# The band's factor on the fourth pair too, shared by GpSimd and VectorE, with the values moved behind the third scores

## What is computed

```
q = (x @ Wq.T + bq + ocr_bias)   k, v likewise     # 16 heads of width 8
scores = q·k / sqrt(8)
scores += 0.1 where |i - j| <= 2, else 0           # the band
attn = softmax(scores)                             # over the 256 keys
out = (attn · v) @ Wo.T + bo
```

## Time and profile before

| | us |
|---|---|
| median of 3 runs | 464.08 |
| the runs | 457.72, 464.08, 465.10 |
| the profiled execution | 460.4 |
| its span | 458.4 |
| mean granted clock | 0.981 |
| TensorE busy in the span | 413.9 (90%) |
| VectorE busy | 348.8 (76%) |
| GpSimd busy | 298.3 (65%) |
| ScalarE busy | 284.8 (62%) |

### The profile page before, as it was taken

One profiled execution on the slowest core, in us unless ns is written; L12 is line 12 of the kernel. 1 busy time (PEld: TensorE's weight loads), 2 busy tenths in 40 slices (PEclk: granted clock), 3 DMA queues, 4 the chain that ended last, 5 costly groups with the idle time before them and its releaser, 6 DMA issues.

```text
span 458.4 us, 11229 instructions
## 1 busy us (share of the span) xinstructions
PE 413.9 (90%) x3804; PEld 265.9 (58%) x3804; DVE 348.8 (76%) x878; ACT 284.8 (62%) x523; POOL 298.3 (65%) x569
## 2 busy tenths in 40 slices
PE   8999789999999998897879888899999999887996
PEld 3555436666666654454447564567667766544674
DVE  5878766888778766996699986767788878367992
ACT  5886424666676676687886448055547575777732
POOL 5523625777777772357899647245676789779962
PEclk9999988999999999899899999989999999999999
DMA  7001876323224100000000006983343332000001
GB/s 215 2 1 49 203 211 166 107 77 85 88 73 104 55 4 1 2 0 2 0 1 2 1 1 165 234 224 93 80 104 107 82 80 56 5 0 1 23 24 46
DMA packets 31123, 31.82 MB, mean 69 GB/s; under 512 B 4953, under 2 KB 26329, under 8 KB 31074
## 3 DMA queue, kind: packets, MB, share of 16 engines
q1 hardware_dynamic: 31074, 31.18, 25.6%
HBM read 21.30 MB, written 9.44 MB: 67 GB/s over the span
## 4 chain that ended last, share of the span: by engine, by line
PE 49%; DVE 18%; POOL 15%; issue 8%; ACT 8%; DVEq 0%; POOLq 0%; ACTq 0%
PE psum L722 6%; ACT h_sb L349 4%; DVE nm L821 4%; POOL hq L1496 3%; PE psum L672 3%; PE psum L675 3%; PE psum L703 3%; PE psum L693 2%; PE psum L673 2%; POOL hb_v L1491 2%; PE psum L726 2%; DVE xn L240 2%; PE psum L694 2%; PE psum L660 2%; DVE nm L824 2%
## 5 line engine op out<-in xcount | busy, mean ns | idle before, releaser
L771 ACT ACTIVATE h_sb<-psum 128x1024 f32<-128x1024 f32 (+1 forms) x128 | 110.9, 914 | 45.9 <-PE psum L694 25.5
L821 DVE TENSOR_REDUCE nm<-psum 128x2 f32<-128x512 f32 x128 | 81.7, 684 | 15.0 <-PE psum L673 14.5
L824 DVE TENSOR_REDUCE nm<-psum 128x3 f32<-128x384 f32 x128 | 65.6, 551 | 10.8 <-PE psum L679 8.9
L781 POOL TENSOR_TENSOR h_sb<-h_sb,bandw 128x512 f32<-128x512 f32 x45 | 57.2, 1271 | 0.0
L246 POOL TENSOR_TENSOR rstd<-veps,mhalf 128x4 f32<-128x4 f32 (+1 forms) x29 | 27.7, 954 | 39.9 <-DVE veps L232 38.8
L722 PE MATMUL psum<-h_sb,v_b 128*32 128x256 f32 x512 | 40.9, 391 | 3.4 <-POOL h_sb L785 1.7
L785 POOL TENSOR_SCALAR_AFFINE_SELECT h_sb<-h_sb 128x512 f32<-128x512 f32 x64 | 40.8, 637 | 0.0
L672 PE MATMUL psum<-kst,qst 72*128 72x256 bf16 x128 | 33.9, 282 | 2.9 <-DMA kst<-k_dram 1.2
L858 DVE RECIPROCAL rsum<-psum 128x16 f32<-128x16 f32 x32 | 8.2, 256 | 33.7 <-PE psum L738 33.7
L675 PE MATMUL psum<-kst,qst 72*128 72x128 bf16 x128 | 29.1, 227 | 5.0 <-DVE nm L824 3.1
L673 PE MATMUL psum<-kst,qst 72*128 72x256 bf16 x128 | 33.3, 276 | 0.0
(11 more groups left out here) (256 smaller groups left out, 1176.2 us busy)
## 6 DMA issues: line engine op xcount, KB each, us to landing
qst<-q_dram SPq DMA_DIRECT2D x96, 96.0 KB
kst<-k_dram SPq DMA_DIRECT2D x96, 96.0 KB
q_dram<-q_parts SPq DMA_DIRECT2D x16, 192.0 KB, 2.6
k_dram<-k_parts SPq DMA_DIRECT2D x16, 192.0 KB, 2.8
k_dram<-k_parts SPq DMA_DIRECT2D x16, 128.0 KB, 2.9
x<-in_L_attn_x SPq DMA_DIRECT2D x4, 256.0 KB, 4.3
out_x<-x SPq DMA_DIRECT2D x4, 256.0 KB, 2.3
pk<-in_packed SPq DMA_DIRECT2D x1, 689.5 KB, 5.9
```

Source lines behind the costliest of these rows:

```text
L771: nc.scalar.activation(pexp[p][:, :, 0:w], psum[:, 4 + 2 * (p % 2):6 + 2 * (p % 2), 0:w], ACT.Exp, scale=scale).then_inc(sem("a_exp"), 1)
L781: ins = nc.gpsimd.tensor_tensor(wide, wide, bandw[:].unsqueeze(1).unsqueeze(1).to_broadcast([P, 2, 2, P]), ALU.mult)
L821: nc.vector.tensor_reduce(nm[slot % 2][:, HEAD[h]], bank[e].rearrange("p (t k) -> p t k", t=2), AX.X, ALU.max, negate=True).then_inc(sem(" ...
L824: nc.vector.tensor_reduce(nm3[slot % 2][:, HEAD[h]], bank[e][:, 0:3 * P].rearrange("p (t k) -> p t k", t=3), AX.X, ALU.max, negate=True).t ...
```

## The change

- `MASKED` becomes (4, 4). Pair 3 of the first attention has 2 products of 256 columns a head, as the others do. The two bf16 copies of the band (`bandm`, `bandm2`) and the ScalarE instructions that make them go.
- GpSimd multiplies the first head of pair 3, behind mask 2 and ahead of the split. VectorE multiplies the second head, one unit later, behind the first pair's maxima (and y) and ahead of the second pair's.
- In unit 15 VectorE does all four pairs; unit 14's second half is in its queue ahead of them.
- The values of group 1 wait for both engines' semaphores, and move behind the third scores.

```diff
-        MASKED = (3, 4)
+        MASKED = (4, 4)
...
-                    if l0 and p < MASKED[inst]:
+                    if l0:
                         nc.tensor.matmul(ps[:, 0:S], k[:, 0:P], q[:, 0:S], start=True, stop=True)
                         last = nc.tensor.matmul(ps[:, S:2 * S], k[:, P:S], q[:, 0:S], start=True, stop=True)
-                    elif l0:
-                        nc.tensor.matmul(ps[:, 0:P + BAND], k[:, 0:P], q[:, 0:P + BAND], start=True, stop=False)
-                        nc.tensor.matmul(ps[:, 0:P + BAND], identb[:], bandm[:], start=False, stop=True)
...
                 if l0 and isinstance(qd, int) and (qd, slot) == last_slot:
-                    pe.wait_ge(sem("a_mskd"), min(2 * g + 2, MASKED[inst]))
+                    pe.wait_ge(sem("a_mskd"), 15 + 2 * g + 2)
                 else:
...
+                    pe.wait_ge(sem("a_msk"), m0 + MASKED[inst] * 4 * (qd - q0) + (MASKED[inst] * slot + 2 * g + 2))
+                    if l0 and g == 1:
+                        pe.wait_ge(sem("a_mskd"), 4 * qd + (slot + 1))
...
+            def banded(p, es):
+                n = es.stop - es.start
+                wide = pexp[p].rearrange("p e (t c) -> p e t c", c=P)[:, es, 0::3]
+                edge = pexp[p][:, :, P:3 * P].rearrange("p e (t c) -> p e t c", c=BAND)[:, es, 0::P - 1]
+                return (wide, bandw[:].unsqueeze(1).unsqueeze(1).to_broadcast([P, n, 2, P]),
+                        edge, bande[:].unsqueeze(1).to_broadcast([P, n, 2, BAND]))
...
                 if l0:
+                    wide, by_wide, edge, by_edge = banded(p, slice(0, 1 if p == 3 else 2))
+                    nc.gpsimd.tensor_tensor(edge, edge, by_edge, ALU.mult)
+                    ins = nc.gpsimd.tensor_tensor(wide, wide, by_wide, ALU.mult)
...
+            def dve_mask(dve, qd, slot, p, es):
+
+                dve.wait_ge(sem("a_exp"), PR * 4 * qd + (PR * slot + p + 1))
+                wide, by_wide, edge, by_edge = banded(p, es)
+                nc.vector.tensor_tensor(edge, edge, by_edge, ALU.mult)
+                nc.vector.tensor_tensor(wide, wide, by_wide, ALU.mult).then_inc(sem("a_mskd"), 1)
...
                         pe_scores(eng, *n2, 1, opening, 2)
-                    if has_prev and l0:
-                        pe_values(eng, *prev, 1)
                     if has_2:
                         pe_scores(eng, *n2, 2, opening, 2)
-                    if has_prev and not l0:
+                    if has_prev:
                         pe_values(eng, *prev, 1)
...
                         dve_y(eng, *yb)
+                    if has_prev and l0:
+                        dve_mask(eng, *prev, 3, slice(1, 2))
                     if has_2:
                         dve_max(eng, *n2, 1)
...
                     if final_band:
-                        dve_mask(eng, 0)
-                        dve_mask(eng, 1)
+                        dve_mask(eng, qd, slot, 0, slice(0, 2))
+                        dve_mask(eng, qd, slot, 1, slice(0, 2))
                     if has_prev:
                         dve_norm(eng, *prev)
                     if final_band:
-                        dve_mask(eng, 2)
+                        dve_mask(eng, qd, slot, 2, slice(0, 2))
+                        dve_mask(eng, qd, slot, 3, slice(0, 2))
```

More of the change, by code:

```diff
@@ L80, in build @@
         identb = sb("identb", [P, P], bf16)
-        bandm = sb("bandm", [P, P + BAND], bf16)
-        bandm2 = sb("bandm2", [P, P + BAND], bf16)
         bandw = sb("bandw", [P, P])
@@ L713, in pe_values @@
                 if l0 and isinstance(qd, int) and (qd, slot) == last_slot:
-                    pe.wait_ge(sem("a_mskd"), min(2 * g + 2, MASKED[inst]))
+                    pe.wait_ge(sem("a_mskd"), 15 + 2 * g + 2)
                 else:
-                    pe.wait_ge(sem("a_msk"), m0 + MASKED[inst] * 4 * (qd - q0) + (MASKED[inst] * slot + min(2 * g + 2, MASKED[inst])))
-                if 2 * g + 2 > MASKED[inst]:
-                    pe.wait_ge(sem("a_exp"), PR * 4 * qd + (PR * slot + 2 * g + 2))
+                    pe.wait_ge(sem("a_msk"), m0 + MASKED[inst] * 4 * (qd - q0) + (MASKED[inst] * slot + 2 * g + 2))
+                    if l0 and g == 1:
+                        pe.wait_ge(sem("a_mskd"), 4 * qd + (slot + 1))
                 out = [bank[2][32 * c:32 * c + 32, 0:S] for c in range(4)]
@@ L771, in act_exp @@
                 nc.scalar.activation(pexp[p][:, :, 0:w], psum[:, 4 + 2 * (p % 2):6 + 2 * (p % 2), 0:w], ACT.Exp, scale=scale).then_inc(sem("a_exp"), 1)
+            def banded(p, es):
[4 more added lines that the diff above has]
+                        edge, bande[:].unsqueeze(1).to_broadcast([P, n, 2, BAND]))
             def pool_mask(pool, qd, slot, p):
-                if p >= MASKED[inst]:
-                    return
                 pool.wait_ge(sem("a_exp"), PR * 4 * qd + (PR * slot + p + 1))
                 if l0:
[L778 to L781, removed]
+                    wide, by_wide, edge, by_edge = banded(p, slice(0, 1 if p == 3 else 2))
+                    nc.gpsimd.tensor_tensor(edge, edge, by_edge, ALU.mult)
+                    ins = nc.gpsimd.tensor_tensor(wide, wide, by_wide, ALU.mult)
                 if not l0:
@@ L1744, in biases @@
                 nc.scalar.activation(maskqk[:], mask_f[:], ACT.Copy)
-                nc.scalar.activation(bandm[:], band_f[:, BAND:P + 2 * BAND], ACT.Copy)
                 nc.scalar.activation(bandw[:], band_f[:, BAND:P + BAND], **gain)
                 nc.scalar.activation(bande[:, 0], band_f[:, P + BAND:P + 2 * BAND], **gain)
-                nc.scalar.activation(bande[:, 1], band_f[:, 0:BAND], **gain)
-                nc.scalar.activation(bandm2[:], band_f[:, 0:P + BAND], ACT.Copy).then_inc(sem("c_masks"), 1)
+                nc.scalar.activation(bande[:, 1], band_f[:, 0:BAND], **gain).then_inc(sem("c_masks"), 1)
                 eng.wait_ge(sem("c_q"), 2)
```

## The result

| | before | changed |
|---|---|---|
| median of 5 runs, us | 463.54 | 492.16 |
| lowest to highest | 457.72 to 465.10 | 486.84 to 502.46 |
| ratio, 95% interval | | 1.0641 (1.0569 to 1.0712) |
| span of the profiled execution | 458.4 | 495.6 |
| mean granted clock, profiled | 0.981 | 0.916 |

The forecast was 478, from 464 to 490; the ratio, here and in the experiments, leaves out executions more than 1.5% above the fastest of their kernel, here the profiled one (497.53) and one of 502.46.

The account below looks back on a forecast made before the run. TensorE's queue was taken to bound each unit. Waits net of shorter products +12.9, units 0, 14 and 15 -0.5 and the stage's end +3 gave +15.4 us; on 462.2 that is 478, range 464 to 490.

Parts of the forecast that it names:

- The wait behind the second scores: TensorE, units 1 to 13: third scores wait for banks, 1.09 us (even) or 1.39 (odd); +12.9 net of shorter products.
- The end of the stage: Units 14 and 15: values of group 1 wait for VectorE's half, and VectorE has more mask work; +3 us, 1.1 to 4.9.
- the wait behind y: Unit 15: VectorE's half is queued behind y, so the values of group 1 start 2.2 us later.
- The shorter products: Pair 3's scores on TensorE: four products replace twelve, saving 0.26 us a unit, 4.2 us at most.
- rival 1: Odd units: VectorE's half loses the SBUF collision and waits for GpSimd's mask; +8.8 us, 487; chance 0.18.
- the term for TensorE's granted clock: TensorE's clock might fall in the third scores' waits; named as a sign of error, not in the sum.
- Rivals 2 and 3: Units' waits: 2, they replace others, 458 us, chance 0.10; 3, about half remains, 469 us, chance 0.12.

Follow-up runs that it names:

- the values back: The changed kernel with only the values of group 1 put back ahead of the third scores: 1.014 of the kernel before, 1.004 when measured again.
- filled kernel: The changed kernel with nine unused identity products a unit in TensorE's waits before and between the third scores' heads: 479.2 us, 1.039 of the kernel before.

## Why the prediction was wrong

The direction was right, the mechanism of the largest term was right and its size a little too large, the time was out of the range by 2 us, and a whole term was missing.

- The wait behind the second scores. Forecast were 1.09 us in even units and 1.39 in odd ones; the trace has 1.10 and 1.33 in units 6 and 5, and 1.13 and 1.24 in units 4 and 3. Two units at full clock were to take 16.2 and take 15.85, 1.65 more than the 14.2 before. The rest is small waits that went: TensorE had stood for about 0.1 us ahead of each unit's transposed maxima, and with the values in front of them it no longer does. That makes +10.7 over 13 units, where 12.9 was worked out.
- The end of the stage. +3 was forecast, from 1.1 to 4.9. With the values back it is 2.8 by the traces and 3.4 by the ratios, by the steps that were named, the wait behind y above all. With the values moved it is more. In the filled kernel the last transposed maxima to the last y take 18.4 us, 3.7 more than before; the two units ahead of that take 14.4 for 12.4, of which one unit's wait explains 0.8. That is 4.9 in all, the forecast's upper bound, and the clock is at the lower level for 7 us of it. What was not seen is that GpSimd's half mask prolongs the hold on the layer norm's scaling.
- The shorter products. 0.26 us a unit, right (two units 14.2 to 13.7).
- VectorE's half and the collision (rival 1). VectorE came first in the odd units as long as the clock was full, and lost twice at half clock, by 2 us in all. Rival 1 is not what took the time past 483. The row that spoke for it was misread: in the earlier trace rows VectorE did not come first by 0.11, since GpSimd's edge had been running from 172.25, before VectorE's 172.30. There too the engine that came first went through.
- The sum with the clock nearly full. The filled kernel at a clock of 0.985 took 473.56, the kernel before at 0.988 on that chip 457.98: +15.6. The sum of the prediction was +15.4. That it agrees so closely is luck: the waits were put 2.2 too high and the end 1.9 too low.
- The step that failed is the term for TensorE's granted clock, which the sum puts at nothing. The last sentence of the prediction names it ("or if TensorE's granted clock falls in these waits, which the stage before doesn't show and the sum doesn't hold"), without a price or a chance. The clock does fall. The reason given was wrong as well, since the kernel before shows it at the lower level within this stage, in unit 0:

```profile
65.50:72.00 6.50, 6.50 (x27) 3.52 (x25) 3.40 (x6) 2.31 (x3) 3.14 (x5) 0.50 0.69 193
```

- The price of the clock. The kernel before's own executions give it: 457.52 us at 0.992 and 465.24 at 0.971, 3.7 us for each 0.01. For the 0.04 lost that is 15 us. Measured are 29.7 (0.0641 × 463.5) less 15.6, so 14.
- Rivals 2 and 3 rested on VectorE catching up. It doesn't: the third scores waited in every unit from 1 to 13, at either level of the clock.

Shown by the runs is that the long stretch at half clock comes with the wait and the shorter products together, with no half on VectorE and no factor on pair 3, that the wait alone brings a smaller one, and that it goes when three products fill the wait. Part of why the clock still varies from 0.97 to 0.99 between executions is a fall at the beginning of the stage, near 65 us: in seven of the thirteen profiled executions it lasts 7 to 14 us, in the other six it is missing. Why it comes in some and not in others stays open, and so does what decides when a stretch at the lower level ends.

## What to carry to other kernels

Products that stand in front of a wait for a bank are cover. Before moving them, take the starts of the instructions that read the bank and count when it comes free. Where TensorE is the slowest engine, a wait in every unit has two prices: its length at full clock, and what the clock takes if it falls; a few idle products put into the wait tell the two apart. A factor moved to another engine at a stage's end also lands in that engine's queue ahead of the next stage's first steps.

## What the runs showed of the hardware

- Waits of 0.73 to 0.95 and 0.37 us, one pair in each unit, with none longer in the 49 us before, preceded a fall of TensorE's granted clock from 1.00 (2.4 GHz) to 0.50 (1.2 GHz) for 34 us; a second stretch of 27 us followed in the same execution. With three idle products a unit the clock stood at 1.00 from 79 to 190 us. The Trainium skill describes the like in "TensorE: Matmul & The Clock Gate", section "A second HAM failure mode: psum-queue depth-cycling": TensorE stands idle briefly between groups of products as it goes round PSUM banks, and the clock goes up and down. The traces here agree in kind, with one or two long stretches at the lower level in the stage, and the filled kernels show the wait for the banks to be the place.
- A VectorE operation on 4 elements from two SBUF tensors took 0.15 us, and 1.09 when it began behind the start of a GpSimd mask. GpSimd's edge took 0.40 for 0.20 when VectorE was first. The hold goes both ways.
